# Attention over 128 heads with a router beside them: the work beside the heads placed by a table, value products in halves, row maxima up to 16 heads ahead

## The reference, cut to what matters

```python
def _L1_attn_ref(x, Wq, Wp, bp):                       # x: 8 sequences, 256 tokens, 16 heads of 16
    q = jnp.einsum('bnhd,hed->bnhe', xh, Wq)
    scores = jnp.einsum('bnhe,bmhe->bhnm', q, q) / NORM
    attn = jax.nn.softmax(scores, axis=-1)
    res = jnp.einsum('bhnm,bmhe->bnhe', attn, q)
    return res.reshape(B, N, D) @ Wp.T + bp
def _route(x_flat, gate_weight, e_bias):               # 2048 tokens, 64 experts in 8 groups
    scores = jax.nn.sigmoid(x_flat @ gate_weight.T)
    sfc = scores + e_bias[None, :]
    group_scores = jax.lax.top_k(sfc.reshape(T, NG, E // NG), 2)[0].sum(-1)
    _, gidx = jax.lax.top_k(group_scores, TG)          # 4 groups, then 8 experts out of them
    ...
h = h + _L1_attn_ref(_layernorm(h), ...)
h = h + _L1_ffn_ref(_layernorm(h), ...)                # mixture of experts, room for 256 rows each
```

## Time and profile before

| what | us |
|---|---|
| median of 3 timed runs | 1216.54 (1217.07, 1210.09, 1216.54) |
| the profiled execution's own time | 1206.56 |
| its span, first to last instruction | 1204.9 |
| PE, DVE, ACT, POOL busy in the span | 1074.5, 753.0, 574.7, 300.6 |
| the 128 turns, first to last exponential | 821.3 to 1003.0 |

### The profile page before, as it was taken

How to read it: one execution, slowest core, us unless ns; L and a number is a source line. 1 busy time by engine, 2 the same in 40 slices (tenths; PEclk the granted TensorE clock), 3 DMA queues, 4 the chain that set the end, 5 groups by cost and what they waited for, 6 DMA issues and landing times. The chain is left out here.

```text
span 1204.9 us, 16311 instructions
## 1 busy us (share of the span) xinstructions
PE 1074.5 (89%) x4812; PEld 705.0 (59%) x4812; DVE 753.0 (62%) x1971; ACT 574.7 (48%) x970; POOL 300.6 (25%) x302
## 2 busy tenths in 40 slices
PE   5899999999999999999999999786988778898761
PEld 4556657656756765765675666653554444477651
DVE  3677775785776676578577683656768854633220
ACT  2572563564365356356435533554665563024430
POOL 6040010010001001001020101224002767347863
PEclk9999999999999999999999999987987978899986
DMA  4300120220121211022170000188432311859875
GB/s 126 127 1 1 49 75 22 84 97 1 48 74 68 72 61 49 0 74 72 67 264 1 18 1 0 26 162 156 88 73 59 109 59 37 297 125 209 153 201 115
DMA packets 58644, 100.07 MB, mean 83 GB/s; under 512 B 12504, under 2 KB 39814, under 8 KB 58315
## 3 DMA queue, kind: packets, MB, share of 16 engines
q1 hardware_dynamic: 40379, 59.22, 18.5%
q0 software_dynamic: 18192, 40.01, 12.2%
HBM read 58.51 MB, written 51.82 MB: 92 GB/s over the span
## 5 line engine op out<-in xcount | busy, mean ns | idle before, releaser
L561 PE MATMUL b_ring<-left 128*128 128x256 f32 x960 | 212.1, 379 | 0.0
L551 PE MATMUL b_ring<-right,left 128*128 128x512 f32 x480 | 208.4, 592 | 0.0
L561 PEld LDWEIGHTS b_ring<-left 128*128 128x128 f32 x960 | 181.4, 190 | 25.0 <-issue 1.0
L1105 POOL TENSOR_TENSOR b_rstd<-b_veps,b_mhalf 128x4 f32<-128x4 f32 x31 | 36.7, 1184 | 558.5 <-DVE b_veps L1179 558.5
L551 PE MATMUL b_ring<-XT,b_wqkv 128*128 128x512 f32 x384 | 170.1, 592 | 0.0
L551 PEld LDWEIGHTS b_ring<-right,left 128*128 128x128 f32 x480 | 91.1, 190 | 114.9 <-issue 103.1
L851 ACT ACTIVATE left<-b_ring,b_cur 128x512 f32<-128x512 f32 x128 | 88.0, 687 | 63.9 <-PE b_ring L551 44.3
L551 PEld LDWEIGHTS b_ring<-XT,b_wqkv 128*128 128x128 f32 x384 | 71.7, 190 | 77.4 <-issue 76.5
L1291 DVE RECIPROCAL b_mixing<-b_mixing 128x1024 f32<-128x1024 f32 x16 | 104.8, 6553 | 0.5
L2561 ACT ACTIVATE a_ET<-a_pB 128x512 f32<-128x512 f32 x128 | 74.3, 595 | 41.9 <-PE a_pB L2298 40.9
L2590 DVE TENSOR_REDUCE nmax<-a_pA 128x2 f32<-128x512 f32 x112 | 74.2, 688 | 32.0 <-PE a_pA L2274 29.8
(11 more groups left out here) (396 smaller groups left out, 1774.5 us busy)
## 6 DMA issues: line engine op xcount, KB each, us to landing
xe<-b_nil POOLq DMA_DIRECT2D x16, 1284.0 KB, 5.9
left<-in_w SPq DMA_DIRECT2D x8, 1024.0 KB, 5.3
a_ET<-xe SPq DMA_DIRECT2D x18, 321.0 KB, 3.7
parts<-in_wexp SPq DMA_DIRECT2D x12, 384.0 KB, 4.1
b_wqkv<-in_wqkv SPq DMA_DIRECT2D x4, 768.0 KB, 4.7
b_rows<-in_rows SPq DMA_DIRECT2D x8, 384.0 KB, 5.3
right<-qparts SPq DMA_DIRECT2D x16, 192.0 KB, 4.9
left<-qparts SPq DMA_DIRECT2D x16, 192.0 KB, 5.2
```

Of the source, the lines that this page charges most:

```text
L551: last = pe.matmul(bank[:, :], lhsT(k), rhs(k), start=(k == 0), stop=(k == n_k - 1))
L561: last = pe.matmul(bank[:, j * D:(j + 1) * D], src[:, k, tile], weights[:, k, :], start=(k == 0), stop=(k == n_k - 1))
```

## The change

The turns of the routing steps come from a table `TURNS` instead of a rule, and the steps are 35 instead of 32: DVE's work of the old steps 18 to 31 is divided anew, with `m_idx` at step 32 and `ksteps` at step 34, PE's `ranks` at step 27 and `taken_counted` at 33. Chunk 0 lies at turns 47 to 87 (before 44 to 75), chunk 1 at 79 to 108 (before 76 to 107), chunk 2 at 109 to 124 (before 108 to 123). `AHEAD` becomes 16, and a sequence's maxima are transposed as early as turn hd = 2 of the sequence before it. `constants` is given out one or two instructions a turn from turn 32 on. `values` and `project` are issued in two halves on neighbouring turns; `add` moves one turn, and its statistics (`summed`) one more. On POOL the factors of chunk 3 come ahead of all scatters of chunk 2.

```diff
-SPAN = 32
+SPAN = 35
+TURNS = (
+    (47, 47, 47, 47, 49, 50, 51, 52, 53, 54, 55, 56, 57, 58, 59, 64, 65, 66,
+     66, 67, 68, 69, 71, 72, 73, 74, 75, 80, 81, 82, 83, 84, 85, 85, 87),
...
-        AHEAD, QRING = 8, 2
+        AHEAD, QRING = 16, 2
...
-            return max(HEADS * (n - 1) + 3 * QUAD, ready + 2)
+            return max(HEADS * (n - 1) + 2, ready + 2)
...
+            return [(l, o) for l in range(ROUTED) for o in range(SPAN) if TURNS[l][o] == step]
...
-                    if l + 1 == ROUTED and j == 2:
+                    if l + 1 == ROUTED and j == 0:
                         rows_measured(l + 1)
...
                 if n > 1:
                     pe.wait_ge(s_nte, n - 1)
-                    pe.wait_ge(s_h, n - 1)
+                if n > 2:
+                    pe.wait_ge(s_h, n - 2)
...
-            def values(i, k):
+            def values(i, k, mt):
...
-                for mt in range(NTS):
-                    for part in range(QUAD):
...
+                for part in range(QUAD):
+                    hd = k * QUAD + part
+                    last = pe.matmul(pO[part * HW:(part + 1) * HW, k % 2, :], qs[:, slot, mt, hd, :],
+                                     ET[:, hd % ERING, mt, :], start=(mt == 0), stop=(mt == NTS - 1))
+                if mt == NTS - 1:
+                    last.then_inc(s_o, 1)
...
-                if i + 1 < SEQS:
-                    pe.wait_ge(s_nte, i + 1)
+                pe.wait_ge(s_nte, min(i + 2, SEQS - 1))
...
-            def project(i):
+            def project(i, nt):
...
-                if o == 25:
+                if o == 27:
                     ranks(l)
-                if o == 30:
+                if o == 33:
                     taken_counted(l)
...
-                    if hd in (7, 11, 15):
-                        values(i, hd // QUAD - 1)
-                    if i and hd == 3:
-                        values(i - 1, QUADS - 1)
+                    if hd >= 6 and hd % QUAD >= 2:
+                        values(i, hd // QUAD - 1, hd % 2)
+                    if i and hd in (2, 3):
+                        values(i - 1, QUADS - 1, hd % 2)
...
-                    if i and hd == 10:
-                        project(i - 1)
+                    if i and hd in (10, 11):
+                        project(i - 1, hd % 2)
...
+            def constants(o):
+                if o == 0:
+                    dve.wait_ge(s_c, 9)
+                    dve.tensor_copy(first[:, :], first_i[:, :]).then_inc(s_cc, 1)
+                if o == 1:
+                    dve.tensor_copy(row[:, :, D], tok_i[:, :]).then_inc(s_cc, 1)
...
-                    if i and hd == 11:
+                    if i and hd == 12:
                         add(i - 1)
+                    if i and hd == 13:
+                        summed(i - 1)
+                    constants(u - 2 * HEADS)
```

More of the change, by code:

```diff
@@ L2300, in shifted @@
                 last.then_inc(s_b, 1)
-            def values(i, k):
+            def values(i, k, mt):
                 n, slot = QUADS * i + k, i % QRING
[L2305 to L2310, removed]
-                for mt in range(NTS):
-                    for part in range(QUAD):
[L2313 to L2316, removed]
+                if mt == 0:
+                    if k == 0:
+                        pe.wait_ge(s_qs, i + 1)
+                        if i < QRING:
+                            pe.wait_ge(s_q1, 2 * (i + 1))
+                    pe.wait_ge(s_ot, n + 2)
+                    pe.wait_ge(s_e, QUAD * (n + 1) + 2)
+                for part in range(QUAD):
[4 more added lines that the diff above has]
+                    last.then_inc(s_o, 1)
             def quad_transposed(i, k):
@@ L2336, in y_transposed @@
                 last.then_inc(s_yt, 1)
-            def project(i):
[L2339 to L2343, removed]
+            def project(i, nt):
+                if nt == 0:
+                    pe.wait_ge(s_yte, i + 1)
+                for k in range(KD):
+                    last = pe.matmul(pH[:, nt, :], yT[:, k, nt * P:(nt + 1) * P], wp[:, k, :], start=(k == 0), stop=(k == KD - 1))
+                if nt == NTS - 1:
+                    last.then_inc(s_p, 1)
             def xn_transposed(l, k):
@@ L2469, in _ @@
                         early_listed(u - LISTED)
-            values(SEQS - 1, QUADS - 1)
+            for mt in range(NTS):
+                values(SEQS - 1, QUADS - 1, mt)
             quad_transposed(SEQS - 1, QUADS - 2)
@@ L2473, in _ @@
             y_transposed(SEQS - 1)
-            project(SEQS - 1)
+            for nt in range(NTS):
+                project(SEQS - 1, nt)
             shared_up(0)
@@ L2480, in _ @@
             shared_up(1)
-            for o in range(14, 27):
+            for o in range(14, 28):
                 routed(ROUTED, o)
             shared_down(1)
-            for o in range(27, SPAN):
+            for o in range(28, SPAN):
                 routed(ROUTED, o)
@@ L2628, in add @@
                 last.then_inc(s_st, 1)
[L2630 to L2645, removed]
-                dve.scalar_tensor_tensor(expert[:, 0, :], upper[:, :], float(-NEXP), expert[:, 1, :], ALU.mult, ALU.add).then_inc(s_cc, 1)
-                dve.wait_ge(s_cc, 13)
-                dve.scalar_tensor_tensor(expert[:, 1, :], expert[:, 0, :], float(SPE), upper[:, :], ALU.mult, ALU.add).then_inc(s_cc, 1)
-                dve.wait_ge(s_cc, 14)
-                dve.tensor_scalar(expert[:, 1, :], expert[:, 1, :], float(-SPE * NEXP), None, ALU.add).then_inc(s_cc, 1)
-                dve.wait_ge(s_cc, 15)
-                dve.wait_ge(s_gw, 32)
@@ L2667, in routed @@
                 if o == 0:
-                    if l == 0:
-                        constants()
                     measured(l)
@@ L2672, in routed @@
                     dve.wait_ge(s_sc, l + 1)
+                    if l == 0:
+                        dve.wait_ge(s_cc, 15)
+                        dve.wait_ge(s_gw, 32)
                     link(dve.tensor_tensor(sfc[:, :, :], score[:, :, :], ebias[:, :].unsqueeze(1).to_broadcast([P, TPC, NEXP]), ALU.add))
@@ L2707, in routed @@
                     link(last)
-                if o == 23:
+                if o == 24:
                     dve.memset(g["carrier"][:, :], 0.0)
@@ L2823, in _ @@
             add(SEQS - 1)
+            summed(SEQS - 1)
             routed(ROUTED, 0)
@@ L2827, in _ @@
             early_listed(2)
-            for o in range(14, 25):
+            for o in range(14, 27):
                 routed(ROUTED, o)
             shared_added(0)
-            for o in range(25, 27):
+            for o in range(27, 29):
                 routed(ROUTED, o)
             shared_hidden(1)
-            for o in range(27, SPAN):
+            for o in range(29, SPAN):
                 routed(ROUTED, o)
```

52 lines of the change are left out of this document (42 added, 10 removed), and 4 rows, old and new, of the table TURNS.

## The result

| kernel | timed runs | median, us | range, us |
|---|---|---|---|
| before | 20 | 1213.64 | 1206.15 to 1217.07 |
| changed | 20 | 1218.28 | 1213.58 to 1222.53 |

The ratio is 1.0044 with a 95% interval of 1.0029 to 1.006. The changed kernel is slower by about 5 us. That is within 1% and within the range I gave, but the forecast's step was -2.0 us and the measured one has the other sign.

What follows compares the result with a forecast made beforehand. POOL's scatters of chunk 0 were taken to hold chunk 2's factors, so quicker turns bring only -2.0: 1206.56 - 2.0 = 1204.5 us profiled, 1214.5 against the timed median of 1216.54; range 1201 to 1224.

Steps and rivals of the forecast that it cites:

- POOL-capped: Forecast's own case: chunk 2's factors wait on POOL for chunk 0's scatters, time within a few us of before; chance 0.58.
- after that: From chunk 2's factors on, the chain between engines and the 201.26 us after the heads stay as before, only shifted.
- from 971.33 to 969.3, -2.0: Start of chunk 2's factors on POOL, behind chunk 0's 30 scatters: 2.0 us earlier than in the profiled execution of before.
- turns 16 to 31: Maxima of 24 heads instead of 16: 19.0 us against 16.56, +2.4; bounds 18.7 and 23.1.
- turns 32 to 47: Constants spread one or two a turn fit into DVE's free time: 17.2 us against 20.05, -2.9.
- turns 48 to 63: Chunk 0's steps 4 to 14; halves and an earlier shift remove little waits: 20.9 us against 22.92, -2.0.
- turns 64 to 79: DVE-bound stretch, DVE's work summing to 21.9 us: 22.5 us against 26.46, -4.0.
- turn 80 to the indices: Six maxima and chunk 0's last routing steps on DVE, up to its indices at turn 85: 7.3 us.
- indices to the factors: POOL: 0.8 us to the first scatter, 38.35 for 30 scatters, 0.3 for row counts, 0.5 to chunk 2's factors.
- no wait for loads: SP: a sequence's 12 loads need at most 14.2 us to issue and land, under the quickest sequence's 16.6; costs nothing.
- scatters held up by DVE: Rival: each of 30 scatters waits for a 0.28 us DVE operation, factors 8.4 us later, 1222.9 us; chance 0.04.
- late indices, and no quicker turns: Rival: dense maxima cost 23.1 us in turns 16 to 31, factors 5.6 us later, 1222 us; chance 0.17.

Runs made afterwards that it cites:

- b_halves: Kernel before with only value products and projection issued in halves; 1212.9 us, ratio 1.0008.
- a_factors: Changed kernel with POOL's factors of chunk 2 moved ahead of the scatters of chunk 0's last tile; 1210.93 us, ratio 0.999 to the kernel before.
- a_whole: Changed kernel with value products of four heads issued whole again, projection still in halves; 1216.88 us, ratio 1.0045 to the kernel before.
- d_best: Kernel before plus table, spread constants, projection in halves and chunk 2's factors ahead of chunk 0's last scatters; 8 heads ahead, whole value products; 1219.05 us, ratio 1.0054.
- b_const: Kernel before with only the constants spread over turns 32 to 48; 1207.72 us, ratio 0.9978, and 0.9996 when run once more.
- c_const_ramp: Kernel before with constants spread and maxima 16 ahead, reached in a slower climb (five heads on four turns); 1212.42 us, ratio 1.0012.
- b_factors: Kernel before with only chunk 2's factors moved ahead of the scatters of chunk 0's last tile on POOL; 1221.03 us, ratio 1.0075.

## Why the prediction was wrong

**What bounds the kernel**: right. The forecast was POOL-capped: the third `m_rstd` comes with no idle time behind the last scatter of chunk 0, ACT's `m_row` at turn 110 waits 9.9 us (5 to 12 were named), and PE stands still there. From the factors to turn 127 it is 31.7 us in both kernels, so "after that" was right as well, and the rest after the heads is 202.10 us against 201.26.

**The step that failed is the sum up to the indices of chunk 0**, on which the factors' step "from 971.33 to 969.3, -2.0" rests. Counted from turn 0 and by the end of `m_idx`, as in the forecast, I had them at 108.1 us; they came at 117.2. The terms, in us:

| term | forecast | measured | late by |
|---|---|---|---|
| turns 16 to 31 | 19.0 | 23.29 | 4.3 |
| turns 32 to 47 | 17.2 | 17.11 | -0.1 |
| turns 48 to 63 | 20.9 | 24.61 | 3.7 |
| turns 64 to 79 | 22.5 | 21.25 | -1.3 |
| turn 80 to the indices | 7.3 | 9.30 | 2.0 |
| indices to the factors | 39.9 | 41.18 | 1.3 |

With 0.3 from sequence 0 that is, but for rounding, the 10.4 us by which the factors came later than forecast (158.4 after turn 0, not 148.0). The mechanism I named was the right one, and two sizes in it, turns 16 to 31 and 48 to 63, were far off. One sum was wrong too: the upper bounds of my own terms, added again, put turn 80 at 932.1 and the factors 8 us later than before, not 6. They came 8.4 later.

*"Two engines nearly equal and coupled through two buffers: I take 19.0."* I took a value 0.3 above the busier engine's sum, when the upper bound, one engine after the other, was 23.1. The four kernels with 24 maxima in that sequence took 22.05 to 24.3 us. The +2.4 became +6.7, in three parts. The halves, which I had put at nothing, are 0.6 (b_halves, 17.18). The eight heads, with the transposes and the `add` that moved beside them, are 4.9, 0.61 each, up to the 22.05 us of a_factors, which has the same program up to there and a clock of 1.00. The last 1.2, up to 23.29, goes with a clock of 0.93 in the changed kernel's profile: PE was busy 20.32 us there and 18.94 in a_factors. So it is the eight heads, 4.9 where I had 2.4, that make 2.5 of the 4.3 us by which the term was low. Sequence 1 of before was no guide: there PE was full and DVE had slack, and in a_factors, with both above 17 us of work, PE's matmuls wait 2.8 us for DVE where before they waited for none. Whether a third buffer for `a_pA` would help wasn't tried.

*Turns 48 to 63: -2.0.* I counted on "little waits" that halves and an early shift would take away. The stretch grew by 1.7 instead, with PE busy 21.31 against 19.95. a_whole, which differs only in the value products, took 22.52 at nearly the same clock, so the halves are about 2 us of it beside the table; the other versions with table and halves took 23.98 to 24.57, the other with the table, spread constants and whole products (d_best) 22.39, at a clock of 1.00. On the kernel before the halves cost nothing there (22.86 against 22.92 in b_halves); why they differ is open. "Dividing `values`, `project` and `add` moves no work off that chain: nothing" was right in the total time and wrong in this stretch. The waits I hoped to save gave little: 22.52 against 22.92.

*Turn 80 to the indices and row counts.* The six maxima and the last steps took 9.3 us, and PE's and DVE's small steps behind them let POOL wait 2.17 us for row counts where I had 0.3.

**Right**: the constants (-2.9, measured -2.94, and b_const by itself gives the same 17.15), the -4.0 for turns 64 to 79 (-5.2), the scatters' pace (1.28 us each beside all that DVE ran here), no wait for loads. The price of the scatters held up by DVE is refuted by these rows.

**The rival "late indices, and no quicker turns"** had sequence 1 at 23.1, the factors 5.6 us later, and 1222. Measured: 23.29, 8.4 later, 1218.28 where before had 1213.64 in the same comparison. It was the right case with a chance of 0.17. It named its deciding point, indices 2 us later than my estimate, and my estimate of sequence 1 alone could be off by 4: a margin smaller than the width of one term should have made the two cases about equally likely. That a profile puts the heads 8.4 us longer and the timed runs the kernel 5 us is not explained; the profiled execution of before, 1206.56 us, was near the lowest of its timed runs (1206.15).

## What to carry to other kernels

Where an in-order queue carries both long batches and short instructions that others wait for, write down when each short one's input is ready and when the batch ahead of it ends; a change that delays the start of the batch by more than the slack turns into a stall downstream, and moving the short one forward costs the same stall at the next one if its input isn't there yet. For two coupled engines with nearly equal work, the sum of the busier one is a lower bound and not an estimate: here an extra item cost 0.6 to 0.8 us, between the slower engine's 0.60 and the serial 0.82, though that engine had 3.4 of the 4.8 us to spare. When a part of a change is taken out to see its price, look for waits that exist only in the mixture: both versions with `AHEAD` 8 had PE wait over 8 us for an `add` that the rest of the change had moved. And put the granted clock beside each stretch before comparing it with the same stretch of another profile.

## What the runs showed that I had not expected

- An early head cost 0.61 to 0.78 us at a clock of 1.00 in sequences 1 and 2 (a_factors against b_halves, c_const_ramp against b_const), though PE's part of it is 0.22 and DVE's 0.60, and hardly less when spread over 32 turns.
- A half value product between two other matmul groups costs 0.67 us of PE and a whole one 1.10: the cost doesn't halve.
- POOL's scatters keep 1.28 us each beside a DVE busy 20.39 of 27.25 us as well as beside an idle one, in all kernels here.
- Stretches of one and the same program differ from profile to profile with the granted clock. Sequence 1 took 23.29 us at 0.93 in the changed kernel and 22.05 at 1.00 in a_factors; it took 17.97 at 0.91 in b_factors and 16.56 at 1.00 in the kernel before.
